# Feed-forward ReLU as one VectorE pass against -bf1, with bf1·Wf2 folded into bf2 by TensorE at the start

## The reference

```
def _norm(x):
    m = jnp.mean(x, axis=-1, keepdims=True)
    s = jnp.sqrt(jnp.mean((x - m) ** 2, axis=-1, keepdims=True))
    return (x - m) / (s + EPS)
...
for i in range(L):                                     # L = 4 layers
    y = _attention(_norm(x), encoder_outputs, dist, bias, Wq[i], ...)   # 16 heads of 64
    x = x + y
    y = jax.nn.relu(_norm(x) @ Wf1[i] + bf1[i]) @ Wf2[i] + bf2[i]       # 128 -> 512 -> 128
    x = x + y
...
x = x + tanh(g_xattn) * _norm(x_after_4_layers)
x = x + tanh(g_ffn) * _L0_ffn_ref(layernorm(x), ...)   # attention and 8 experts
```

## Time and profile before

| | us |
|---|---|
| median of 3 runs | 1382.73 (1380.3 to 1384.69) |
| the profiled execution, its own time | 1388.81 |
| its span in the trace | 1387.1 |
| PE, DVE, ACT, POOL busy | 1228.3, 1222.8, 1064.8, 834.8 |

### The profile page before, as it was taken

How to read it: one execution, slowest core, us unless ns; L and a number is a source line. 1 busy time by engine, 2 the same in 40 slices (tenths; PEclk the granted TensorE clock), 3 DMA queues, 4 the chain that set the end, 5 groups by cost and what they waited for, 6 DMA issues and landing times.

```text
span 1387.1 us, 39817 instructions
## 1 busy us (share of the span) xinstructions
PE 1228.3 (89%) x11184; PEld 1013.8 (73%) x11184; DVE 1222.8 (88%) x4922; ACT 1064.8 (77%) x3353; POOL 834.8 (60%) x889
## 2 busy tenths in 40 slices
PE   1599989898989899898989898989898999788897
PEld 1377878787878787777878787878787878666665
DVE  4899989898989999898989898989898988579996
ACT  4588878787878888787878686878787876568886
POOL 3677767676767677676767676767676754211110
PEclk9899999999999999999999999999999999989999
DMA  5201000002110000021100101111101000000000
GB/s 153 67 7 30 16 27 12 29 12 76 44 31 12 23 19 22 20 68 34 31 25 13 29 12 31 57 47 28 31 12 42 12 12 9 5 22 19 18 20 9
DMA packets 69117, 41.06 MB, mean 30 GB/s; under 512 B 14841, under 2 KB 63873, under 8 KB 68993
## 3 DMA queue, kind: packets, MB, share of 16 engines
q1 hardware_dynamic: 68992, 39.84, 10.1%
HBM read 23.29 MB, written 1.05 MB: 18 GB/s over the span
## 4 chain that ended last, share of the span: by engine, by line
issue 27%; DVE 24%; ACT 18%; PE 17%; POOL 3%; DVEq 1%; DMA 1%; ACTq 0%; SPq 0%; POOLq 0%
ACT prob L802 10%; DVE bias_acc L951 4%; PE M L582 3%; ACT relu_z L785 3%; PE O L552 3%; DVE score L998 3%; DVE qT L1123 3%; DVE hid L1073 3%; DVE st L1016 2%; PE M L628 2%; PE M L560 2%; PE L L689 1%; ACT probT L809 1%; ACT oT L814 1%; DVE rs L1025 1%
## 5 line engine op out<-in xcount | busy, mean ns | idle before, releaser
L802 ACT ACTIVATE prob<-score,nmax 128x128 f32<-128x128 f32 x1024 | 396.7, 390 | 182.7 <-DVE nmax L998 177.3
L1396 POOL TENSOR_TENSOR prob<-prob,rinv 128x512 f32<-128x512 f32 x256 | 293.9, 1148 | 234.0 <-DVE rinv L1006 231.9
L951 DVE SCALAR_TENSOR_TENSOR bias_acc<-relu_z,cst,bias_acc 128x512 f32<-128x512 f32 x370 | 339.7, 918 | 9.7 <-ACT relu_z L785 0.2
L785 ACT ACTIVATE relu_z<-dist_g,cst 128x512 f32<-128x512 f32 x386 | 294.9, 804 | 16.9 <-DMA cst<-cst_all 16.9
L998 DVE CUSTOM_DVE_ANT_0 score<-L,bias 128x128 f32<-128x128 f32 x1024 | 233.8, 282 | 4.2 <-PE L L528 1.5
L802 ACT ACTIVATION_READ_ACCUMULATOR prob<-score,nmax 128x1 f32 x1024 | 193.2, 189 | 0.0
L1391 POOL TENSOR_TENSOR sd<-mv,half 128x1 f32<-128x1 f32 x128 | 105.6, 825 | 120.4 <-DVE mv L1018 117.6
L538 PE MATMUL T<-ident,prob 128*128 128x128 f32 x1024 | 163.9, 284 | 4.7 <-POOL prob L1396 3.8
L552 PEld LDWEIGHTS O<-probT,v 128*64 128x64 f32 x2048 | 109.3, 136 | 62.0 <-issue 54.4
L582 PE MATMUL M<-wv,ctxT 128*128 128x512 f32 x256 | 147.0, 658 | 7.7 <-DVE hid L1073 5.1
L528 PE MATMUL L<-kT,qT 64*128 64x128 f32 x2048 | 149.6, 286 | 0.0
(11 more groups left out here) (134 smaller groups left out, 2226.7 us busy)
## 6 DMA issues: line engine op xcount, KB each, us to landing
dist_g<-in_fside_BxSxS SPq DMA_DIRECT2D x16, 256.0 KB, 2.7
mask_g<-in_mask_Bx1x1xS_ff SPq DMA_DIRECT2D x16, 256.0 KB, 3.5
ctxT<-ctxT_all SPq DMA_DIRECT2D x64, 64.0 KB, 1.9
xs<-x_all SPq DMA_DIRECT2D x64, 64.0 KB, 1.8
x_all<-xs SPq DMA_DIRECT2D x64, 64.0 KB, 1.9
wk<-in_L_xattn_Wk SPq DMA_DIRECT2D x4, 512.0 KB, 3.7
wv<-in_L_xattn_Wv SPq DMA_DIRECT2D x4, 512.0 KB, 4.3
wq<-in_L_xattn_Wq SPq DMA_DIRECT2D x4, 512.0 KB, 5.0
```

Source lines behind the costliest of these rows:

```text
L785: nc.scalar.activation(relu_z[:, z_slot(g, k), :], dist_g[:, :, :], ACT.Relu, bias=cst[:, C_BTH + k:C_BTH + k + 1], scale=cst[:, C_WTH + k ...
L802: last = nc.scalar.activation(prob[:, c, m, :], score[:, c, m, :], ACT.Exp, bias=nmax[:, c, m:m + 1], scale=-1.0, accum_out=rsum[:, c, m:m ...
L951: vec.scalar_tensor_tensor(out=bias_acc[:, :], in0=relu_z[:, z_slot(g, k), :], scalar=weight, in1=bias_acc[:, :], op0=ALU.mult, op1=ALU.ad ...
L1396: gp.tensor_tensor(prob[:, c, :, :], prob[:, c, :, :], rinv[:, c, :].rearrange("p (m o) -> p m o", o=1).broadcast_to([P, 4, P]), ALU.mult) ...
```

## The change: what it does

It uses relu(y + b) = max(y, -b) + b. The first part is one VectorE instruction over 128 x 512; the second part, b, goes through Wf2 as a constant row per layer, bf1·Wf2, which is added to bf2.

- **VectorE, per unit:** the four `tensor_scalar` become one `tensor_tensor` (max) of M1 with `nb1c`, a 128 x 4 tile of -bf1, broadcast along 128 columns.
- **SyncE, opening:** three more loads after Wq: Wf2 of all layers (1 MB, into `prob`), bf1 of all layers (2048 elements of 4 bytes), bf2 of all layers broadcast to 128 partitions. `load_b1` and `load_b2` copy from SBUF tiles; for layer 0 they stand where they stood, each behind a new wait: for ScalarE's negation (`fold_rep`) and for VectorE's sum (`fold_kept`).
- **ScalarE, end of step(0, -1):** -bf1 of all layers (128 x 16), and bf1 broadcast to 128 x 2048 (into `score`).
- **TensorE, end of step(0, -1):** 16 matmuls 128 x 128 x 128 into M2, four per layer. One more wait in step(0, 0).
- **VectorE, end of step(0, -1), behind `finish_bias(0, 0)`:** wait for these matmuls, one 128 x 512 sum of M2 and bf2.
- Some semaphores of the last part are no longer made in pairs, of which one was unused; the waits are the same.

```
+            sp.dma_start(wf2_all, Wf2.rearrange("l (c p) d -> p (l c) d", p=P)).then_inc(fold_in, 16)
+            sp.dma_start(bf1_all[:, :], bf1.rearrange("l (c p) -> p (l c)", p=P), allow_slow_non_contiguous=True).then_inc(fold_in, 16)
+            sp.dma_start(bf2e_all[:, :, :], bf2.rearrange("(o l) d -> o l d", o=1).broadcast_to([P, LAYERS, P])).then_inc(fold_in, 16)
             sp.wait_ge(cT_kept, 4)
             load_ctx_slot(0, 0)
...
             load_f2(0)
+            sp.wait_ge(fold_rep, 1)
             load_b1(0)
+            sp.wait_ge(fold_kept, 1)
             load_b2(0)
 
             sp.dma_start(gates_in[:, 0:1], g_xattn.rearrange("(o n) -> o n", o=1).broadcast_to([P, 1])).then_inc(f_gate_in, 16)
...
             def load_b1(l):
-                sp.dma_start(bf1c[:, :], bf1[bass.ds(l, 1), :].rearrange("l (c p) -> p (l c)", p=P), allow_slow_non_contiguous=True).then_inc(w_b1, 16)
+                sp.dma_start(nb1c[:, :], nb1_all[:, l * (FILT // P):(l + 1) * (FILT // P)]).then_inc(w_b1, 16)
 
             def load_b2(l):
-                sp.dma_start(bf2b[:, :], bf2[bass.ds(l, 1), :].broadcast_to([P, P])).then_inc(w_b2, 16)
+                sp.dma_start(bf2b[:, :], bf2e_all[:, l, :]).then_inc(w_b2, 16)
...
+            def fold_biases():
+
+                pe.wait_ge(fold_in, 48)
+                pe.wait_ge(fold_rep, 2)
+                pe.wait_ge(hT_kept, 1)
+                for l in range(LAYERS):
+                    for c in range(FILT // P):
+                        last = mm(M2[:, l * P:(l + 1) * P], b1_rep[:, l * (FILT // P) + c, :], wf2_all[:, l * (FILT // P) + c, :],
+                                  start=c == 0, stop=c == FILT // P - 1)
+                last.then_inc(fold_done, 1)
...
                 if cur:
                     apply(g, i, 0)
-
+                if isinstance(g, int) and g == 0 and i == -1:
+                    fold_biases()
...
+                if isinstance(g, int) and g == 0 and i == -1:
+                    act.wait_ge(fold_in, 48)
+                    nc.scalar.activation(nb1_all[:, :], bf1_all[:, :], copy, scale=-1.0).then_inc(fold_rep, 1)
+                    nc.scalar.activation(b1_rep, bf1_all[:, :].rearrange("p (n o) -> p n o", o=1).broadcast_to([P, LAYERS * (FILT // P), P]),
+                                         copy).then_inc(fold_rep, 1)
...
-                    for c in range(FILT // P):
-                        if c == 0:
-                            dve.wait_ge(f1_done, after(g, i - 2, 1))
-                            wait(dve, f2_done, after(g, i - 4, 1))
-                            if i % GROUP == 2:
-                                dve.wait_ge(w_b1, layer_of(g, i - 2) * 16 + 16)
-                        last = vec.tensor_scalar(hid[:, i % 2, c, :], M1[:, c * P:(c + 1) * P], bf1c[:, c:c + 1], 0.0, ALU.add, ALU.max)
-                    last.then_inc(hid_kept, 1)
+                    dve.wait_ge(f1_done, after(g, i - 2, 1))
+                    wait(dve, f2_done, after(g, i - 4, 1))
+                    if i % GROUP == 2:
+                        dve.wait_ge(w_b1, layer_of(g, i - 2) * 16 + 16)
+
+                    vec.tensor_tensor(hid[:, i % 2, :, :], M1[:, :].rearrange("p (c t) -> p c t", c=FILT // P),
+                                      nb1c[:, :].rearrange("p (c o) -> p c o", o=1).broadcast_to([P, FILT // P, P]),
+                                      ALU.max).then_inc(hid_kept, 1)
...
                 if i == -1:
                     finish_bias(0, 0)
+                    dve.wait_ge(fold_done, 1)
+                    vec.tensor_tensor(bf2e_all[:, :, :], M2[:, :].rearrange("p (l d) -> p l d", l=LAYERS), bf2e_all[:, :, :],
+                                      ALU.add).then_inc(fold_kept, 1)
```

More of the change, by code:

```diff
@@ L185, in block_program @@
         xb = sb("xb", [P, 2, P])
+        wf2_all = prob[:, :, :, :].rearrange("p c m t -> p (c m) t")
+        b1_rep = score[:, :, :, :].rearrange("p c m t -> p (c m) t")
         gates_in = sb("gates_in", [P, 2])
@@ L257, in block_program @@
         f1_done, hid_kept, f2_done = sem("f1_done"), sem("hid_kept"), sem("f2_done")
+        fold_in, fold_rep, fold_done, fold_kept = [sem("fold_" + n) for n in ("in", "rep", "done", "kept")]
         f_consts, f_in, f_gate_in, tanh_done = sem("f_consts"), sem("f_in"), sem("f_gate_in"), sem("tanh_done")
@@ L261, in block_program @@
         out_st = [sem(f"out_st{i}") for i in range(2)]
-        fbn, fvar, fve, fsd, fsde, frs, frg = [[sem(f"f{n}{a}") for a in "ab"] for n in ("bn", "var", "ve", "sd", "sde", "rs", "rg")]
+        fbn, fvar, fsd, frs = [[sem(f"f{n}{a}") for a in "ab"] for n in ("bn", "var", "sd", "rs")]
+        fve, fsde, frg = [sem(f"f_{n}") for n in ("ve", "sde", "rg")]
         fdelta, fx1, fh, fhT_done, fhT_kept = [sem("f_" + n) for n in ("delta", "x1", "h", "hT_done", "hT_kept")]
@@ L635, in step @@
                     wait(pe, h2T_kept, after(g, i - 2, 1))
+                    if isinstance(g, int) and g == 0 and i == 0:
+                        pe.wait_ge(fold_kept, 1)
                     nc.tensor.transpose(M2[:, 0:P], h[:, (i + 1) % 2, :], ident[:, :]).then_inc(hT_done, 1)
@@ L1155, in f_first @@
                     dve.wait_ge(fsd[0], after(g, i, 1))
-                    vec.tensor_scalar(t[:, 1:2], t[:, 0:1], NORM_EPS, None, ALU.add).then_inc(fsde[0], 1)
+                    vec.tensor_scalar(t[:, 1:2], t[:, 0:1], NORM_EPS, None, ALU.add).then_inc(fsde, 1)
                 elif part == 3:
-                    dve.wait_ge(fsde[0], after(g, i, 1))
+                    dve.wait_ge(fsde, after(g, i, 1))
                     vec.reciprocal(t[:, 2:3], t[:, 1:2]).then_inc(frs[0], 1)
@@ L1161, in f_first @@
                     dve.wait_ge(frs[0], after(g, i, 1))
-                    vec.tensor_tensor(t[:, 3:4], t[:, 2:3], tg[:, 0:1], ALU.mult).then_inc(frg[0], 1)
+                    vec.tensor_tensor(t[:, 3:4], t[:, 2:3], tg[:, 0:1], ALU.mult).then_inc(frg, 1)
                 elif part == 5:
-                    dve.wait_ge(frg[0], after(g, i, 1))
+                    dve.wait_ge(frg, after(g, i, 1))
                     wait(dve, fx1, after(g, i - 2, 1))
@@ L1182, in f_first @@
                     wait(dve, fsd[1], after(g, i - 2, 1))
-                    vec.tensor_scalar(t[:, 4:5], mvF[:, 1, s, 1:2], LN_EPS, None, ALU.add).then_inc(fve[1], 1)
+                    vec.tensor_scalar(t[:, 4:5], mvF[:, 1, s, 1:2], LN_EPS, None, ALU.add).then_inc(fve, 1)
                 elif part == 10:
@@ L1493, in f_root @@
                     pool.wait_ge(fvar[0], after(g, i, 1))
-                    wait(pool, fsde[0], after(g, i - 2, 1))
+                    wait(pool, fsde, after(g, i - 2, 1))
                     gp.tensor_tensor(tinyF[:, s, 0:1], mvF[:, 0, s, 1:2], half[:, 0:1], ALU.pow).then_inc(fsd[0], 1)
                 else:
-                    pool.wait_ge(fve[1], after(g, i, 1))
+                    pool.wait_ge(fve, after(g, i, 1))
                     wait(pool, frs[1], after(g, i - 2, 1))
```

7 lines of the change are left out of this document (5 added, 2 removed).

## The result

| | before | after |
|---|---|---|
| median, us | 1383.71 (4 runs, 1380.3 to 1386.45) | 1419.38 (4 runs, 1415.89 to 1421.38) |
| the profiled execution, its span | 1388.81, 1387.1 | 1419.82, 1418.1 |
| mean granted clock of TensorE | 0.970 | 0.954 |

The account below looks back on a forecast made before the run. VectorE was taken to lead the cycle, TensorE a few tenths behind. From the profiled 1388.8 us, -18 (loop) + 15 (opening) gave 1385.8; as the median lies 6.1 below that execution, the forecast was 1380 us, range 1368 to 1392.

Parts of the forecast that it names:

- The price of the new pass: VectorE's ReLU: one pass of 0.69 us, 0.61 to the next start, against 1.05 for four; saves 0.44 us a unit.
- What of it reaches the end: gain 18 us: Main loop: TensorE's waits cap VectorE's saving; units give 0, 0.44, 0.31, 0.44 us a pass, 18 us gained overall.
- No change after 1131 us but the shift: Sign of being right: after 1131 us the kernel would only move in time; 0 us of change there.
- nothing at the jump that I can price: VectorE's loop jump: fewer instructions in the loop body were given no priced effect.
- The opening: Fold and SyncE's queue behind it: group 1's relu_z starts at 74 instead of 58; net 15 us lost (11 to 19).
- the three loads: Opening, after Wq: 1.3 MB more takes 3.8 us, small pieces perhaps 1; delay taken as 0.5 us (0 to 2).
- B: Rival, 24%: the opening costs more than the loop gives; 19 us lost at SyncE's wait, loop gains 12; 1390 us.
- A: Rival, 20%: VectorE's whole saving counts in the loop; 28 us gained, 15 lost, 1370 us.

Follow-up runs that it names:

- e4: The changed kernel with 36 short memsets at the start of VectorE's stream; 1392.74 us, ratio 1.0064 to the kernel before.
- e2: The fold alone: the changed kernel with the four ReLU passes put back, on the tile of -bf1; 1395.91 us, ratio 1.0088.
- e1: The one pass alone: the kernel before with the single max pass and no fold; 1392.28 us, ratio 1.0058.
- e15: The kernel before with 29 short memsets ahead of VectorE's stream and nothing else; 1388.58 us, ratio 1.0047.
- e12: The changed kernel with 18 short memsets ahead of VectorE's stream; 1394.62 us, ratio 1.0063.
- e16: The kernel before with 93 short memsets ahead of VectorE's stream and nothing else; 1420.38 us, ratio 1.0266.
- e11: The changed kernel with 36 memsets, scores of heads 4 to 7 ahead of the inverse, and the whole fold moved behind the opening; 1385.55 us, ratio 1.0006.
- e14: The kernel before with the one pass, no fold, 37 memsets, GpSimd's bias terms thinned to 16 of 512 columns except the first group; 1354.14 us, ratio 0.9796.
- e5: e4 with the scores of heads 4 to 7 ahead of the inverse of heads 0 to 3; 1391.32 us, ratio 1.0058.
- e8: The kernel before with the scores of heads 4 to 7 ahead of the inverse of heads 0 to 3; 1408.70 us, ratio 1.0180.
- e17: The kernel before with 222 short memsets at the start of VectorE's stream; 1414.97 us, ratio 1.0240.
- e18: The kernel before with 247 short memsets at the start of VectorE's stream; 1438.47 us, ratio 1.0411.

## Why the prediction was wrong, point by point

Forecast: 1380 (1368 to 1392). Measured: 1419.4, 39.4 over. By the terms: the loop 21.6 (a gain of 18 forecast, 3.6 lost), the last part 10.8 (0 forecast), the opening 1.6 (15 forecast, 16.6 lost), and 5.7 because the profiled execution that the sum started from lay 6.1 us over its median and that of after 0.4 over its own. Together 39.7; the 0.3 too much is the rounding of 1379.7 to 1380.

- **The price of the new pass: right.** 683 ns, 0.60 us to the next start (0.61 forecast), 0.44 us saved a unit. By the rule that I quoted from the Trainium skill ("VectorE: DVE Perf Modes", The DRAIN you can't avoid) it would be 0.66. The same section adds that a next instruction that is not held starts earlier, which I had left out; these rows, 0.60 to the next start for 0.68 of work, agree with that.
- **"What of it reaches the end: gain 18 us": this is the step that failed.** I took TensorE's waits for VectorE as what the unit would shrink by, as if VectorE's own stream were free to move up. Two things spoke against it, and I could have had both: ScalarE's exponentials of the first heads depend on scores made ahead of the ReLU, so nothing behind the next inverse can come sooner by way of VectorE; and the mean of 918 ns for a bias term hid two prices, 0.8 alone and 1.3 beside GpSimd. In the loop the gain was under 1 us at equal clock (e4 against e2, e1 against e15), by the medians 2.3 and 3.2 in all.
- **"No change after 1131 us but the shift" and "nothing at the jump that I can price": these failed too.** Fewer instructions on VectorE moved both loops to worse places in its stream. After against e4 that is 15.0 us behind the last h2T copy and 10.7 in the loop (4.1 of these are the waits of 0.3 us a pass, most of the rest goes with 10.2 us more at 1.2 GHz), 26.6 in all by the medians: more than the gain of 18 and the 15 of the opening that I had priced, each by itself. e4, e12 and e16 show it.
- **The opening: right in kind, size and place.** The fold's matmuls 5.84 us (5.5 forecast), `fold_kept` 66.4 (63.8), distances issued 72.09 (70.4), relu_z at 75.77 (74). The term behind the 1.7 us too few is the three loads: I had put the small pieces at 1 us and the delay at 0.5, but the load of bf1's 2048 pieces of 4 bytes holds SyncE's queue for 4.76 us and bf2's for 3.42 (in e11, where they stand behind the ten loads, 1.77 and 3.24), the contexts go out 3.8 us later, and ScalarE comes to the fold's copy at 57.8.
- **The rivals.** B's side came true but not its mechanism: its opening would have cost 19 and its loop gained 12. No rival had the stall. A (the whole saving counts) came true by half where GpSimd was thinned (e14), and in full only with the exchange (e5 against e8), where the dearer terms cost as much.
- **The range** was too narrow since every term in it was a price of work. None was a price of where an instruction stands.

## What to carry to other kernels

Before costing a saving on the busiest engine, follow the next instruction there that waits for another engine, and ask whether what it waits for also moves up; if it hangs on work ahead of the saving, the saving ends there. A mean over a group of equal instructions may be two prices, one alone and one beside another engine: split it by what runs beside it. And when an edit changes the number of instructions in front of a loop, compare the "issue" waits at its jumps first; some short instructions ahead of the stream tell in one run whether a loss is work or place.

## What the runs showed that I had not expected

- The place of a loop in VectorE's stream is worth up to 4% of this kernel. The last loop (325 instructions) stalls 4.7 to 5.1 us at its jump from instruction 1467, 1468, 1595 and 1724, 2.7 from 1531, not at all from 1485, 1503, 1504 and 1749; 1724 lies 256 behind 1468, and 1749 256 behind the middle of 1485 to 1503, where there is no stall either. The main loop's jump costs 2.4 to 2.5 us at best and 3.5 in e16 and e17; e18 pays twice.
- Two bias terms of VectorE take 2.60 us beside GpSimd's passes and 1.62 alone, and no view counts that as a wait.
- After each loop head, where TensorE idles for some 3.5 us, it is granted 1.2 GHz for 3.4 us, and at some heads for 6.8; such a pass takes 73.2 to 74.2 us in after instead of 71.9 to 72.5. What decides between one stretch and two stays open. It was not tried by itself; two heads had a second stretch in before, three in after, none in e4, which differs from after by the memsets and their tile alone.
